# Last chunk's experts with Silu on ScalarE, weights spread by TensorE, and a new order of the instructions

## What is computed

```python
x = x + attention(layernorm(x))            # heads 16 x 8, layernorm of q and k, rope, causal softmax
xf = layernorm(x)
scores = softmax(xf @ gate_w.T)            # then + gate_b, best 2 of 4 groups, best 2 experts
combine = (one_hot(idx, 16) * weights[..., None]).sum(1)
h = silu(xf @ We1 + be1) * (xf @ We3 + be3)       # every expert, for every token
y = einsum('te,ted->td', combine, h @ We2 + be2)
z = silu(xf @ ws1 + bs1) * (xf @ ws3 + bs3) @ ws2 + bs2
x = x + y + z
```

## Time and profile before

| | |
|---|---|
| median of three runs | 418.56 us |
| the three runs | 415.84, 418.56, 419.45 us |
| span of the profiled execution | 414.9 us |
| granted TensorE clock, mean | 0.954 |

### The profile page before, as it was taken

One profiled execution on the slowest core, in us unless ns is written; L12 is line 12 of the kernel. 1 busy time (PEld: TensorE's weight loads), 2 busy tenths in 40 slices (PEclk: granted clock), 3 DMA queues, 4 the chain that ended last, 5 costly groups with the idle time before them and its releaser, 6 DMA issues.

```text
span 414.9 us, 8178 instructions
## 1 busy us (share of the span) xinstructions
PE 352.3 (85%) x2999; PEld 153.8 (37%) x2999; DVE 314.9 (76%) x619; ACT 267.0 (64%) x395; POOL 151.3 (36%) x182
## 2 busy tenths in 40 slices
PE   2563388998989899999889999889887899999994
...
GB/s 95 223 181 128 24 16 139 5 2 116 43 3 1 3 207 75 104 2 0 1 73 135 28 2 3 2 2 1 2 2 4 2 2 130 78 0 0 30 202 25
DMA packets 26424, 21.69 MB, mean 52 GB/s; under 512 B 9201, under 2 KB 22162, under 8 KB 26322
## 3 DMA queue, kind: packets, MB, share of 16 engines
...
## 4 chain that ended last, share of the span: by engine, by line
PE 45%; DVE 35%; ACT 6%; issue 6%; DMA 3%; POOL 2%; SPq 2%; DVEq 0%; ACTq 0%; POOLq 0%
PE psum L687 14%; PE psum L666 8%; DVE mx_diag L1072 7%; DVE mx_full L1072 6%; PE psum L733 5%; PE psum L614 5%; PE psum L640 4%; PE psum L722 4%; ACT probs L795 4%; PE psum L596 4%; DVE mv L1144 2%; DVE nr L1012 2%; POOL mh L994 2%; DVE nr L1011 2%; DMA comb_b<-combine_scratch 2%
## 5 line engine op out<-in xcount | busy, mean ns | idle before, releaser
L795 ACT ACTIVATE probs<-psum 128x1024 f32<-128x1024 f32 x144 | 141.0, 1021 | 51.1 <-PE psum L614 29.9
L1072 DVE TENSOR_REDUCE mx_diag<-psum 128x4 f32<-128x512 f32 (+2 forms) x96 | 95.7, 1038 | 19.0 <-PE psum L640 17.9
L1072 DVE TENSOR_REDUCE mx_full<-psum 128x2 f32<-128x1024 f32 x64 | 75.6, 1217 | 16.9 <-PE psum L640 16.7
L994 POOL TENSOR_TENSOR mh<-mh,mv 128x512 f32<-128x512 f32 x36 | 45.2, 1269 | 93.0 <-DVE mv L1144 93.0
L687 PE MATMUL psum<-probs,v_ones 128*9 128x512 f32 (+3 forms) x768 | 77.4, 492 | 0.5 <-ACT probs L795 0.4
L722 PE MATMUL psum<-x2T,w 128*128 128x512 f32 x144 | 69.1, 606 | 1.5 <-ACT mv L832 0.8
L666 PE MATMUL psum<-q_st,k_st 64*128 64x512 bf16 (+3 forms) x384 | 53.8, 327 | 11.8 <-ACT probs L795 6.0
L640 PE MATMUL psum<-k_st,q_st 62*128 62x512 bf16 (+3 forms) x384 | 58.2, 337 | 4.1 <-ACT probs L795 2.5
L614 PE MATMUL psum<-masks 64*128 64x128 bf16 (+2 forms) x896 | 51.0, 213 | 11.8 <-DVE mx_diag L1072 9.2
L614 PEld LDWEIGHTS psum<-masks 64*128 64x128 bf16 x896 | 32.3, 95 | 45.6 <-DVE mx_diag L1072 23.2
L1144 DVE SCALAR_TENSOR_TENSOR mv<-psum,b,mv 128x512 f32<-128x512 f32 x36 | 26.3, 746 | 30.1 <-ACT mh L844 30.0
...
## 6 DMA issues: line engine op xcount, KB each, us to landing
...
xs<-in_x SPq DMA_DIRECT2D x3, 256.0 KB, 10.9
...
```

What stands on the lines that cost most here:

```text
L795: act.activation(probs[:, n % P_RING, :, :], wpair("scores", (s, i)), ACT.Exp, scale=SCALE).then_inc(exp_done, 1)
L994: pool.tensor_tensor(t, t, mv[:, at % V_RING, :], ALU.mult).then_inc(gate_done, 1)
L1072: dve.tensor_reduce(dst[:, a % 2, qt, :, pairs[0]:pairs[0] + nm], w, AX.X, ALU.max, negate=True).then_inc(max_free, 1)
```

## The change

Chunk 3's experts are computed in another way. `moeG` and `moeL` take the place of `moeU` and `moeV`. ACT takes Silu of the gate part with its bias straight into `mv` (`moe_s`), and DVE makes (linear + bias) times that in one pass into `mh` (`moe_m`); there is no work for POOL. The combine weights of chunk 3 don't go through DRAM: DVE splits them in three bf16 parts (`comb3`), PE turns the 48 columns (`cT3`), ACT copies them (`cT3_read`), and for each unit one bf16 product with a constant of zeros and ones (`pick`, 48 rows) adds the three parts up in fp32 and spreads them over the 64 rows of each expert (`wide`). `moe_h_dve` multiplies `mh` by that PSUM bank. The turned fp32 weights (`cT.3`) are still made, for the bias. `comb_b` shares its space with early tiles, so chunk 0's loads wait for the last rope. The whole list `ORDER` is new; stages of the other chunks and of attention are the same ones, in another order and with other banks. The diff, with the lists cut:

```diff
-WEIGHT_OF = ("moe_h", "moe_h", "moe_h", "moe_h_dve")
+LAST = NX - 1
+SPLIT = 3
...
+pv.78 pv.79 oT.14@4 moeV.2.5@5 leave.15 oT.15@2 moe_v.2.5 moeU.2.3@1 moe_t.2.3 oT_read.14 oT_read.15 moe_a.2.2 onT.3@4
+onT_read.3 moeU.2.4@5 moeV.2.6@2 proj.3@4 moe_h.2.1 moe_g.2.2 moe_h.2.2 moe_v.2.6 moe_a.2.3 moe_g.2.3 moeV.2.7@3
+proj_read.3 moe_t.2.4 moe_a.2.4 moeU.2.5@0 norm2.3 moe_t.2.5 moe_a.2.5 moeU.2.6@2 cload.2.3 moeU.2.7@4 moe_g.2.4
+moe_g.2.5 moeV.2.8@5 moe_y.2.0 moe_y.2.1 moe_y.2.2 moe_t.2.6 moe_a.2.6 moe_v.2.7 moe_t.2.7 moe_a.2.7 norm2_apply.3
+moe_v.2.8 x2T.3@3 x2T_read.3 moeU.2.8@2 moe_g.2.6 cload.2.1 gate.3@3 gate_read.3 moe_t.2.8 moe_a.2.8 moeL.3.0@1
+gate_exp.3 moe_h.2.3 moeG.3.0@5 moe_s.3.0 moeG.3.1@4 moe_y.2.3 moe_s.3.1 moe_h.2.4 moe_y.2.4 moe_h.2.5 moe_y.2.5
+moe_g.2.7 moeG.3.2@4 moe_s.3.2 moeL.3.1@0 moe_g.2.8 route1.3 route2.3 moe_h.2.6 moe_h.2.7 store.1 moe_h.2.8 moe_y.2.6
+moe_m.3.0 moeG.3.3@4 moe_s.3.3 moeL.3.2@3 moeL.3.3@1 moeG.3.4@5 moe_m.3.1 moe_s.3.4 moe_y.2.7 moe_y.2.8 y_leave.2
+moeL.3.4@0 moe_m.3.2 moeG.3.5@4 moeG.3.6@2 moeG.3.7@6 route3.3 comb3.3 moe_s.3.5 moe_s.3.6 moe_m.3.3 cT3.3@5 yturn.2@1
+final.2 moe_s.3.7 moeL.3.5@4 cT3_read.3 moe_m.3.4 moe_m.3.5 wide.3.1@6 moeG.3.8@1 moe_s.3.8 moe_h_dve.3.1 cT.3@0
+wide.3.2@2 moe_h_dve.3.2 moeL.3.6@5 moeL.3.7@4 moe_m.3.6 moe_m.3.7 moe_y.3.0 wide.3.3@2 moe_h_dve.3.3 wide.3.4@3
+moe_h_dve.3.4 wide.3.5@5 wide.3.6@4 cT_read.3 moe_h_dve.3.5 moe_y.3.1 moe_y.3.2 moe_y.3.3 moe_y.3.4 wide.3.7@2
+wide.3.8@5 moeL.3.8@1 store.2 moe_h_dve.3.6 moe_y.3.5 moe_y.3.6 moe_h_dve.3.7 moe_m.3.8 moe_h_dve.3.8 moe_y.3.7
+moe_y.3.8 y_leave.3 yturn.3@0 final.3 store.3
...
+            sp.dma_start(pick[:, :, :].rearrange("p u r -> p (u r)").bitcast(F32), c_pick).then_inc(ld_moe, 16)
...
-                    if x >= 1:
+                    if x == 0:
+                        sp.wait_ge(roped_ready, NX)
+                    else:
                         sp.wait_ge(weighted, PAIRS * (x - 1) + 2 * part + 2)
...
+            def combine_parts_turn(x):
+                w = fill("cT3", x).bitcast(BF16)
+                pe.wait_ge(comb3_ready, 1)
+                for t in range(TPC):
+                    last = pe.transpose(w[0:SPLIT * E, t * P:(t + 1) * P], comb3[:, t, :, :].rearrange("p s e -> p (s e)"),
+                                        ident_bf[:, :])
+                last.then_inc(work_full, 1)
+
+            def weights_over_rows(x, n):
+                w = fill("wide", (x, n))
+                pe.wait_ge(work_read_act, frees("act", turned("cT3", x)))
+                pe.matmul(w, pick[:, unit(n), :], comb3T[:, :], start=True, stop=True).then_inc(work_full, 1)
...
+            def moe_silu(x, n):
+                at = UNITS * x + n
+                act.wait_ge(work_full, turned("moeG", (x, n)))
+                if n < V_RING:
+                    act.wait_ge(gate_done, at - V_RING + 1)
+                else:
+                    act.wait_ge(u_read, at - V_RING + 1)
+                act.activation(mv[:, at % V_RING, :], wbank("moeG", (x, n)), ACT.Silu,
+                               bias=b1[:, unit(n):unit(n) + 1]).then_inc(work_read_act, 1)
...
+            def linear_unit(x, n):
+                at = UNITS * x + n
+                dve.wait_ge(work_full, turned("moeL", (x, n)))
+                dve.wait_ge(work_read_act, frees("act", turned("moeG", (x, n))))
+                dve.wait_ge(y_done, at - T_RING + 1)
+                dve.scalar_tensor_tensor(out=mh[:, at % T_RING, :], in0=wbank("moeL", (x, n)), scalar=b3[:, unit(n):unit(n) + 1],
+                                         in1=mv[:, at % V_RING, :], op0=ALU.add, op1=ALU.mult).then_inc(u_read, 1)
+
+            def combine_parts(x):
+                c = lg[:, 11, :, :]
+                dve.wait_ge(comb_ready, x + 1)
+                link(dve.tensor_copy(comb3[:, :, 0, :], c))
+                link(dve.tensor_tensor(comb_left[:, :, :], c, comb3[:, :, 0, :], ALU.subtract))
+                link(dve.tensor_copy(comb3[:, :, 1, :], comb_left[:, :, :]))
+                dve.tensor_tensor(comb3[:, :, 2, :], comb_left[:, :, :], comb3[:, :, 1, :], ALU.subtract).then_inc(comb3_ready, 1)
...
                 elif kind == "moe_h_dve":
-                    if WEIGHT_OF[arg[0] - 1] != kind and arg[1] == 1:
-                        dve.wait_ge(weighted, PAIRS * arg[0])
-                    weight(dve, *arg)
+                    x, n = arg
+                    at = UNITS * x + n
+                    dve.wait_ge(work_full, turned("wide", arg))
+                    dve.wait_ge(u_read, at + 1)
+                    h = mh[:, at % T_RING, :]
+                    dve.tensor_tensor(h, h, wbank("wide", arg), ALU.mult).then_inc(work_read_dve, 1)
```

More of the change, by code:

```diff
@@ new lines @@
+scores.15.1@45 scores.16.0@23 scores.16.1@01 exp.15.1 exp.16.0 pv.12 exp.16.1 max.7.5@45 stack.2.0.2 qT_low.3
+scores.17.0@23 exp.17.0 pv.13 pv.14 norm2.0 max.8.0@23 max.8.1@01 maxred.7.5 max.8.2@45 maxred.8.0 maxred.8.1
+norm2_apply.0 x2T.0@6 leave.4 pv.15 x2T_read.0 gate.0@6 mrow.6 maxred.8.2 gate_read.0 gate_exp.0 max.8.3@01 max.8.4@23
+moeV.0.0@5 maxred.8.3 maxred.8.4 moeU.0.0@6 route1.0 moeV.0.1@4 oT.4@2 oT_read.4 moe_v.0.0 moe_t.0.0 moeV.0.2@5
+moe_a.0.0 moe_v.0.1 moe_v.0.2 scores.18.0@01 max.8.5@23 max.8.6@45 maxred.8.5 maxred.8.6 moeU.0.1@6 exp.18.0 max.8.7@01
@@ new lines @@
+cload.0.0 moe_g.0.3 moe_v.0.7 moeV.0.8@2 moe_a.0.5 max.8.11@45 moe_g.0.4 maxred.8.11 moe_v.0.8 max.8.12@01
+scores.21.1@23 exp.21.1 maxred.8.12 moeU.0.6@4 oT.5@6 max.8.13@23 maxred.8.13 scores.22.0@01 moe_t.0.6 exp.22.0
+moeU.0.7@5 moe_t.0.7 mmin.8 cload.0.1 moe_a.0.6 moe_a.0.7 scores.22.1@23 scores.23.0@01 mneg.8 mturn.8@4 oT_read.5
+mcopy.8 exp.22.1 pv.19 pv.20 leave.6 mrow.8 max.9.0@45 moe_h.0.1 max.9.1@23 moeU.0.8@6 exp.23.0 maxred.9.0 cload.0.2
+maxred.9.1 pv.21 max.9.2@45 moe_t.0.8 moe_a.0.8 scores.24.0@01 scores.24.1@23 pv.22 pv.23 maxred.9.2 exp.24.0 exp.24.1
```

270 lines of the change are left out of this document (137 added, 133 removed).

## The result

The changed kernel takes 400.76 us (median of four runs, 400.11 to 402.67); the kernel before, run beside it, 417.20 (414.33 to 419.45). The ratio is 0.962, with a 95% interval of 0.957 to 0.967. The forecast was 411.5 and its range began at 402.5: the sign was right, the gain was more than twice what I had worked out, and it lies just outside the range. The profiled execution after has a span of 400.9 us at a mean granted clock of 0.945, so the profiles differ by 14.0 us, and that is what has to be explained. (It was the slowest of the four, so its 14.0 is less than the 16.4 between the medians.)

What follows compares the result with a forecast made beforehand. The prediction took the kernel to be near PE's work, with gains only where PE idles. Tail -0.4, x2T.3 -1.2, front -1.5 and middle -4.0 gave -7.1 on 414.9, so 407.8, plus 3.7: 411.5 us, range 402.5 to 421.

Steps and rivals of the forecast that it cites:

- the step from span to median: Adding 3.7 us, the median run's time over the profiled span, to turn the forecast span of 407.8 into 411.5.
- What bounds the kernel: PE is busy 85% of the span, so a change is worth what it saves where PE idles; 12.6 us from 240 to 335.
- Middle, -4.0: Rest of the new order: fewer tight bank refills -2.5, chunk 1's combine weights -1.5; bounds -9 to +9 us.
- x2T.3 itself, -1.2: Before x2T.3: moeU.2.8 and y.2.3 moved behind it, 1.7 us less; a Tanh ahead of onT_read.3, +0.5; bounds -2.2 to +1.5.
- Chunk 1's weights, -1.5: Part of the middle: 8.5 us of PE work instead of 5.2 between cT.1 and moe_h.1.1 covers POOL's load wait; -1.5 us.
- Front, -1.5: Halved and headsum.2 go behind the first maxima, so the first maximum starts 2.3 us earlier; only part lasts; -2.3 to 0.
- Tail, -0.4: From x2T.3 to the end: 39.9 us instead of 40.3, set by PE's work, not the DRAM round trip; bounds -2, +2.5.
- the sign of a stall that I missed: Stated sign of a wrong forecast: a tail from x2T.3 to the end of over 43 us.
- The rival in which DVE decides: Tail: DVE's 32.4 us sets it, as PE's products overlap more than counted; gain 6 instead of 0.4, 406 us; chance 0.12.
- The table load: Second ACT_TABLE_LOAD, 1.3 us, before the first Silu, covered by 8.4 us of router passes on DVE: 0, +1.3 if uncovered.
- The slower rival, POOL's queue: Maxima splits (mneg) of groups 8 to 11 wait among POOL's expert products: +16.4 us, no middle gain, 424.7 us; chance 0.18.

Runs made afterwards that it cites:

- s4: Changed kernel with the old list only between the read of x2T.2 and x2T.3: 410.48 us, 0.9846 of before.
- s1: Changed kernel with the old list only from gate_read.0 to x2T.1, chunk 0's experts crowded ahead of x2T.1: 417.11 us, 0.9998 of before.
- e1: Kernel before (Tanh, chunk 3's weights through DRAM) with the new list up to x2T.3 and an old-manner tail: 399.26 us, 0.957 of before.
- b1: Changed kernel with the DRAM scratch of the combine weights at its old size of four chunks: 400.69 us.
- t3: Changed kernel, list behind x2T.3 reordered, POOL's last four weight products of chunk 2 held back by two waits: 398.15 us, 0.9549 of before.
- l3: Changed kernel with the old list up to x2T.3 and the new list and computing of chunk 3 behind it: 420.25 us, 1.0051 of before.

## Why the prediction was right and wrong

**The sum.** In spans the forecast was 407.8 and the result 400.9, so 6.9 us too much: the front gave 0.6 less than I had said, the time from there to x2T.3 12.8 more (18.0 instead of 5.2), and the tail 5.3 less. The other 3.8 us of the miss are in the step from span to median. I had added 3.7; in every run on record the time is only 1.8 over its own span, and the profiled execution after was the slowest of its four. The forecast's 3.7 held the luck of which execution was profiled.

**What bounds the kernel.** Right, and the one view that mattered was there: PE's busy time did not change, its idle time did, and the largest stock of idle time was from 240 to 335, where I said that no engine is full.

**Middle, -4.0: the step that failed.** Measured on the same cut: PE's idle time in stretches 2 to 4 went from 19.3 to 5.5, so -13.8. The mechanism was named, the term was sized at less than a third. Two parts of it went wrong in different ways. I had counted 24 refills with under 1.0 us of work between them against 8, had found "up to 8 us" for the sixteen, and then took a third of it because "another reader often steps in". Stretch 4, the later part of that range, gave 6.9 by itself, and 8.2 by putting the old list back there (s4). I should have taken the whole: the wait of the earlier trace rows was there, 35.7 us long, and no row spoke for the third. The other part I had on the wrong side. I wrote that the experts of chunks 0 and 1 "are spread and end late" and booked it as a danger. Stretch 3, where chunk 0's now end, lost 6.1 us of idle time. Their sums are PE work that can be done at any time, and the new list keeps them for behind x2T.1. That they are what took the idle time away is argued, not shown: s1, which spends them earlier, lost 16.3 us, but in part by its seam. So the cause in stretch 3 stays open.

**x2T.3 itself, -1.2.** It did not come. From the end of the last `pv` (341.6) to x2T.3 (355.71) it took 14.1 us, as the 13.8 of before: moeU.2.8 and y.2.3 are gone from there, but moeU.2.3 and 2.4 stand there now.

**Chunk 1's weights, -1.5.** Wrong, and of no weight. POOL still waits for their load, 7.75 us instead of the 5.93 of the earlier trace rows:

```profile
211.99 2.51 POOL L484 TENSOR_TENSOR mh<-mh,early 128x512 f32<-128x512 f32 x2 [7.75 <-DMA early<-combine_scratch]
```

PE idles 0.6 of the 20 us around it (195 to 215), because it has other sums and maxima. A wait of an engine that is a third busy should have been no term of the sum.

**Front, -1.5.** The mechanism held and the sum did not. The list gives -4.7 (e1), three times what I took; the first maximum, which I put near 48, starts there at 46.9. The changed code takes 3.8 back, most likely by the late load, which no step of mine contained: its first maximum started at 50.74.

**Tail, -0.4: wrong side.** From x2T.3, which now starts at 355.71, to the end it took 45.2 us, not 39.9, and not the 40.3 of before. That is over the 43 which I had named as the sign of a stall that I missed. The difference to the forecast is 5.3. The stop of PE is 2.2 of it and the slow clock behind it 1.8 (2.72 and 2.88 for what takes 1.88 each; this part comes and goes, b1 has the stop without it). The rest is the bf16 products of `wide`: I took 0.24 us each, with bounds 0.1 and 0.39. In the changed kernel PE works from 380.24 to 396.08 without a stop; fourteen fp32 products at 0.87 and one turn at 0.53 leave 3.1 us for eight of them, 0.39 each, 1.2 more in all. What I said of the structure held: PE's work and not DVE's sets the tail, once the router is quick (t3). The forecast of 39.9 was 42.3 there. Against the old tail the new computing is worth 1.4 us as made (e1 46.1, after 44.7), and with the old list ahead nothing (l3 41.4 and s4 39.6, before 39.6). In t3 it is 4.5, but e1's router is held up by POOL too, and an old tail with POOL held was not run. The rival in which DVE decides did not come. Its price was also wrong by its own terms: 32.4 instead of 40.3 is 7.9 less, not 6.

**The table load.** Right: one second load, 1.28 us at 358.77, ahead of the first Silu and beside the router, with no one waiting for it. Of the drain of about 1380 ns that the prediction took from the Trainium skill ("ScalarE: Activation LUTs", where the figure stands in "What ACT_TABLE_LOAD costs"), nothing shows: the first Silu starts 0.02 us after the load's end.

```profile
358.77 1.28 ACT L884 ACT_TABLE_LOAD   x1
360.07 1.27 ACT L884 ACTIVATE mv<-psum,b 128x512 f32<-128x512 f32 x2
```

Silu takes 0.687 us as the Tanh row said, the linear pass 0.746, the product with a PSUM tile 0.684.

**The slower rival, POOL's queue,** did not happen: mneg.10 found POOL idle, and PE's idle time in stretch 3 is 2.9.
